# Cross attention in a two-layer decoder: six rounds a row of four 125-key units, in place of eight rounds of one head pair

## The reference

```python
Q = (x @ Wq.T).reshape(B, xN, NUM_HEADS, HEAD_DIM)
KV = (z @ Wkv.T).reshape(B, zN, 2, NUM_HEADS, HEAD_DIM)
attn = jnp.einsum('bqhd,bkhd->bhqk', Q, K) * SCALE
attn = jax.nn.softmax(attn, axis=-1)
O = jnp.einsum('bhqk,bkhd->bqhd', attn, V).reshape(B, xN, DIM)
return O @ Wo.T
```

## Time and profile before

| | |
|---|---|
| median of 3 runs | 1423.16 us |
| profiled execution, its own time | 1427.28 us |
| its span | 1425.5 us |
| PE busy, PEld busy | 1253.4 us (88%), 1003.8 us (70%) |
| DVE, ACT, POOL busy | 703.0, 556.0, 444.4 us |
| first cross attention, second | about 153 to 468 us, 918 to 1226 us |

### The profile page before, as it was taken

The page is one execution under the profiler, slowest core; times in us unless marked ns, Lnnn a source line. Parts: engine busy times, 40 slices in busy tenths (PEclk is TensorE's granted clock), DMA queues, the critical chain, the costliest instruction groups (busy, mean ns, idle before and its releaser), DMA issues. The chain is left out here.

```text
span 1425.5 us, 34481 instructions
## 1 busy us (share of the span) xinstructions
PE 1253.4 (88%) x13524; PEld 1003.8 (70%) x13524; DVE 703.0 (49%) x1744; ACT 556.0 (39%) x1246; POOL 444.4 (31%) x654
## 2 busy tenths in 40 slices
PE   5999799999998199999994999789999999469996
PEld 2666467777776199999993777556777776369996
DVE  4786545555553622222222999655555555512332
ACT  2777145555554022222221555235555555112221
POOL 5986300000000246566552222200000000146562
PEclk9999799999999599999997999789999999779998
DMA  7000111111110379999994000011111111469993
GB/s 248 2 3 1 24 31 34 38 37 37 40 38 14 136 274 335 343 345 347 323 348 111 1 1 1 11 29 32 45 44 45 43 47 35 103 227 350 359 367 140
DMA packets 61355, 177.89 MB, mean 125 GB/s; under 512 B 20608, under 2 KB 41953, under 8 KB 46756
## 3 DMA queue, kind: packets, MB, share of 16 engines
q0 software_dynamic: 22176, 141.55, 27.8%
q1 hardware_dynamic: 39044, 34.46, 9.4%
HBM read 147.62 MB, written 12.85 MB: 113 GB/s over the span
## 5 line engine op out<-in xcount | busy, mean ns | idle before, releaser
L1010 DVE TENSOR_REDUCE xa_mx<-xa_ps_s 112x2 f32<-112x750 f32 x246 | 231.5, 941 | 215.0 <-PE xa_ps_s L710 202.7
L927 ACT ACTIVATE xa_p<-xa_ps_p 125x672 f32<-125x672 f32 x244 | 178.2, 730 | 216.5 <-PE xa_ps_p L716 216.5
L716 PEld LDWEIGHTS xa_ps_p<-xa_qT,xa_kT 32*125 32x125 f32 x2928 | 184.8, 186 | 88.5 <-ACT xa_p L927 54.6
L716 PE MATMUL xa_ps_p<-xa_qT,xa_kT 32*125 32x112 f32 x2928 | 225.8, 285 | 21.9 <-DVE xa_mx L1010 10.0
L710 PE MATMUL xa_ps_s<-xa_kT,xa_qT 32*112 32x375 f32 x984 | 222.2, 528 | 2.1 <-DVE xa_mx L1010 2.1
L1842 PEld LDWEIGHTS ex_ps_h<-ex_xT,ew_w 128*128 128x128 f32 x1792 | 213.4, 196 | 4.8 <-issue 2.0
L1842 PE MATMUL ex_ps_h<-ex_xT,ew_w 128*128 128x128 f32 x1792 | 213.9, 279 | 1.3 <-ACT ex_xT L1872 1.3
L1853 PE MATMUL ex_ps_y<-ew_w,ex_hT 128*128 128x256 f32 x896 | 202.7, 380 | 0.0
L1853 PEld LDWEIGHTS ex_ps_y<-ew_w,ex_hT 128*128 128x128 f32 x896 | 166.2, 190 | 20.0
L1876 ACT ACTIVATE ex_hT<-ex_ps_h,ew_w 128x128 f32<-128x128 f32 x224 | 69.9, 363 | 281.9 <-PE ex_ps_h L1842 281.9
L1888 DVE TENSOR_SCALAR ex_hT<-ex_ps_h,ew_w 128x128 f32<-128x128 f32 x224 | 68.3, 347 | 163.4 <-PE ex_ps_h L1842 163.4
(11 more groups left out here) (305 smaller groups left out, 1977.5 us busy)
## 6 DMA issues: line engine op xcount, KB each, us to landing
xa_kT<-xa_kU SPq DMA_DIRECT2D x128, 93.8 KB, 2.2
xa_qT<-xa_qU SPq DMA_DIRECT2D x64, 56.0 KB
xn<-xa_x SPq DMA_DIRECT2D x32, 112.0 KB, 2.2
lin_yg<-ys SPq DMA_DIRECT2D x16, 224.0 KB, 5.7
cT<-in_ctxT SPq DMA_DIRECT2D x4, 750.0 KB, 8.3
xa_qT<-xa_nmT SPq DMA_DIRECT2D x128, 1.8 KB
x<-in_x SPq DMA_DIRECT2D x4, 448.0 KB, 5.8
xn<-x SPq DMA_DIRECT2D x16, 112.0 KB, 2.1
```

Of the source, the lines that this page charges most:

```text
L716: return pe.matmul(shifted_banks(b, pair)[0:CT, i, c * S:(c + 1) * S], kT[r:r + 32, b % RB, n, c * CT:(c + 1) * CT], qT[r:r + 32, b % RB, ...
L927: act.activation(p[slot % 4][:, :, :], shifted_banks(t, slot)[0:CT, :, 0:NC3 * S], ACT.Exp).then_inc(exped, 1)
L1010: dve.tensor_reduce(mx[:, b % 2, j:j + 2, n], score_banks(b, pair)[0:S, :, 0:CL], AX, ALU.max).then_inc(maxed, 1)
```

## The change

- A row has six rounds. A round takes four units of 125 keys from each of two strips: `unit(slot, u)` numbers the twelve (quad, chunk) units of a strip, four to a slot. `score` multiplies one unit (125 columns) and no longer all 375; `shifted_score` is the product it was, eight to a round in place of six. `exps` covers 2 x 448 columns, into one of six tiles `p`.
- `maximum` leaves a maximum for each unit (48 a query), and `shift_rows` has a second reduction (`top`) from 48 to 16, ahead of the negation.
- `values` runs two groups at a time: 0 and 1 after round 4, 2 and 3 after round 0 of the next row, with a round on either side.
- The whole-array work stands after rounds 1, 2, 3 and 5. `logits` writes to bank `bm` and not to `bk`, so `keys` no longer waits for VectorE's `row_logits`; `finish` runs one row earlier. `queries` and the first `keys` are a row further ahead, and SP's spreading with them.
- The work ahead of the loop is written out anew: `x_turn(1)`, `queries(1)` and `keys(1, 0)` stand before the first `fill_round`; nine fill rounds in place of eleven.

```diff
-    PAIRS = H // 2
+    ROUNDS, UNITS = 6, 4
...
+    p = [ph.sb(f"p{r}", [CT, 2, UNITS * S]) for r in range(ROUNDS)]
+    mx = ph.sb("mx", [S, 2, 4, QUADS * NC3])
+    top = ph.sb("top", [S, H])
...
+    AHEAD = 3
+    FILL = ROUNDS + AHEAD
+    DRAIN = ROUNDS * NB - FILL
+    EXPED = (2, 4, 6, 6)
...
+    def unit(slot, u):
+
+        k = UNITS * (slot // 2) + u
+        return k // NC3, k % NC3
...
+                n, c = unit(slot, u)
+                return pe.matmul(score_banks(b, slot)[0:S, i, u * CT:(u + 1) * CT], qT[r:r + 32, b % RB, n, :],
+                                 kT[r:r + 32, b % RB, n, c * CT:(c + 1) * CT], start=True, stop=True)
...
             def round_of(t, slot):
                 sb, sp = ahead(t, slot)
...
+                    spread_waits(sb, sp)
+                    r = ROUNDS * sb + sp
+                    pe.wait_ge(maxed, r)
+                for u in range(UNITS):
+                    if on(t):
+                        for i in range(2):
+                            last = shifted_score(t, slot, i, u)
+                        if u == UNITS - 1:
+                            last.then_inc(shifted, 1)
+                    if on(sb):
+                        for i in range(2):
+                            last = score(sb, sp, i, u)
+                        if u == UNITS - 1:
+                            last.then_inc(scored, 1)
...
+                    k = NC3 * n + c
+                    u = k % UNITS
                     for j in range(4):
+                                         p[2 * (k // UNITS) + j // 2][:, j % 2, u * S:(u + 1) * S], start=(c == 0), stop=(c == NC3 - 1))
...
             def x_turn(b):
                 pe.wait_ge(x_normed, b + 1)
...
                 reused(pe, nm_copied, b - 1)
...
             def logits(b):
                 pe.wait_ge(x2_t, b + 1)
+                pe.wait_ge(x_summed, min(b + 2, NB))
...
-                    last = pe.matmul(bk[0:S, 2 * P:2 * P + NE], x2T[:, c, :], g.wr[:, layer, c, :], start=(c == 0), stop=(c == 1))
+                    last = pe.matmul(bm[0:S, 2 * P:2 * P + NE], x2T[:, c, :], g.wr[:, layer, c, :], start=(c == 0), stop=(c == 1))
...
             def keys(b, m):
+                reused(pe, k_copied, 2 * b + m)
                 if m == 0:
-                    reused(pe, k_copied, 2 * b)
-                    reused(pe, lg_set, b - 4)
-                else:
-                    reused(pe, v_copied, NC3 * b)
-                    pe.wait_ge(k_copied, 2 * b + 1)
+                    reused(pe, v_copied, NC3 * (b - 2) + 2)
+                    reused(pe, x2_t, b - 4)
...
             for t in range(NB + 2):
                 round_of(t, 0)
                 if on(t - 1):
+                    values(t - 1, 2)
                     values(t - 1, 3)
-                if on(t + 2):
-                    keys(t + 2, 0)
...
                 round_of(t, 1)
-                if on(t + 2):
-                    queries(t + 2)
-                round_of(t, 2)
-                if on(t):
-                    values(t, 0)
-                if on(t - 1):
-                    u_turn(t - 1)
-                round_of(t, 3)
-                if on(t + 1):
-                    context_values(t + 1, 0)
-                    context_values(t + 1, 1)
-                round_of(t, 4)
-                if on(t):
-                    values(t, 1)
-                if on(t + 1):
-                    context_values(t + 1, 2)
-                round_of(t, 5)
                 if on(t + 2):
                     keys(t + 2, 1)
                 if on(t + 1):
-                    shift_turn(t + 1)
-                round_of(t, 6)
-                if on(t):
-                    values(t, 2)
+                    context_values(t + 1, 0)
+                if on(t - 1):
+                    u_turn(t - 1)
+                round_of(t, 2)
+                if on(t + 1):
+                    context_values(t + 1, 1)
+                    context_values(t + 1, 2)
                 if on(t - 1):
                     out_turn(t - 1)
-                if on(t - 2):
-                    row_turn(t - 2)
-                round_of(t, 7)
-                if on(t + 3):
-                    x_turn(t + 3)
+                round_of(t, 3)
+                if on(t + 1):
+                    shift_turn(t + 1)
                 if on(t - 1):
                     out_product(t - 1)
                 if on(t - 2):
+                    row_turn(t - 2)
+                if on(t + 3):
+                    x_turn(t + 3)
+                round_of(t, 4)
+                if on(t):
+                    values(t, 0)
+                    values(t, 1)
+                round_of(t, 5)
+                if on(t + 3):
+                    queries(t + 3)
+                    keys(t + 3, 0)
+                if on(t - 2):
                     logits(t - 2)
...
-                act.wait_ge(shifted, PAIRS * t + slot + 1)
-                reused(act, valued, 4 * t + slot // 2 - 1)
-                act.activation(p[slot % 4][:, :, :], shifted_banks(t, slot)[0:CT, :, 0:NC3 * S], ACT.Exp).then_inc(exped, 1)
+                act.wait_ge(shifted, ROUNDS * t + slot + 1)
+                reused(act, valued, 4 * t - (2 if slot < 2 else 0))
+                act.activation(p[slot][:, :, :], shifted_banks(t, slot)[0:CT, :, 0:UNITS * S], ACT.Exp).then_inc(exped, 1)
...
                     out_copy(t - 1)
+                if on(t):
+                    exps(t, 3)
+                if on(t + 1):
+                    shift_copy(t + 1)
                 if on(t - 2):
                     row_copy(t - 2)
                 if on(t + 3):
                     x_copy(t + 3)
+                if on(t):
+                    exps(t, 4)
+                    exps(t, 5)
+                if on(t + 3):
+                    k_copy(t + 3, 0)
...
+            def maximum(b, slot):
+                dve.wait_ge(scored, ROUNDS * b + slot + 1)
+                j, k = 2 * (slot % 2), UNITS * (slot // 2)
+                made = score_banks(b, slot)[0:S, :, 0:UNITS * CT].rearrange("t i (u k) -> t i u k", u=UNITS)
+                dve.tensor_reduce(mx[:, b % 2, j:j + 2, k:k + UNITS], made, AX, ALU.max).then_inc(maxed, 1)
...
             def shift_rows(b):
-                dve.wait_ge(maxed, PAIRS * (b + 1))
+                dve.wait_ge(maxed, ROUNDS * (b + 1))
+                made = mx[:, b % 2].rearrange("t j (n c) -> t (j n) c", c=NC3)
+                dve.tensor_reduce(top[:, :], made, AX, ALU.max).then_inc(topped, 1)
...
+                    if slot == 1 and on(t - 2):
                         second_norm(t - 2)
...
+                    if slot == 2 and on(t + 1):
                         shift_rows(t + 1)
+                    if slot == 3 and on(t - 1):
+                        finish(t - 1)
+                    if slot == 5 and on(t + 3):
+                        q_copy(t + 3)
+                    if slot == 5 and on(t - 2):
+                        row_logits(t - 2)
...
```

More of the change, by code:

```diff
@@ L731, in round_of @@
[L731 to L734, removed]
-                if on(t):
-                    for i in range(2):
[L737 to L740, removed]
-                if on(t):
[L742 to L745, removed]
@@ L756, in values, with fill_round @@
+            def fill_round(b, slot):
+                spread_waits(b, slot)
+                reused(pe, maxed, ROUNDS * b + slot - 1)
+                for u in range(UNITS):
+                    for i in range(2):
+                        last = score(b, slot, i, u)
+                last.then_inc(scored, 1)
             def values(b, n):
-                pe.wait_ge(exped, PAIRS * b + 2 * n + 2)
+                pe.wait_ge(exped, ROUNDS * b + EXPED[n])
                 if n == 0:
@@ L828, in u_turn @@
                 reused(pe, x_summed, b)
+                reused(pe, lg_set, b - 1)
                 for n in range(QUADS):
@@ L857, in _ @@
             keys(0, 1)
+            x_turn(1)
             bias_rows()
-            idle_products(bp[:, 0, 0:P], 5 + 4 * layer)
+            queries(1)
+            keys(1, 0)
+            idle_products(bp[:, 0, 0:P], 2)
             fill_round(0, 0)
             fill_round(0, 1)
-            x_turn(1)
-            keys(1, 0)
+            keys(1, 1)
+            context_values(0, 0)
             fill_round(0, 2)
             fill_round(0, 3)
-            queries(1)
+            context_values(0, 1)
+            context_values(0, 2)
             fill_round(0, 4)
             fill_round(0, 5)
-            context_values(0, 0)
-            context_values(0, 1)
-            fill_round(0, 6)
-            fill_round(0, 7)
-            context_values(0, 2)
-            keys(1, 1)
+            fill_round(1, 0)
             shift_turn(0)
-            for pair in range(FILL - PAIRS):
-                fill_round(1, pair)
+            keys(2, 0)
             x_turn(2)
+            fill_round(1, 1)
+            fill_round(1, 2)
+            queries(2)
             for t in range(NB + 2):
@@ L970, in _ @@
```

(27 more changed lines are left out.)

172 lines of the change are left out of this document (73 added, 99 removed).

## The result

The changed kernel takes 1389.91 us (median of 4 runs, 1389.60 to 1390.92) against 1424.91 (1421.94 to 1428.47): a ratio of 0.9755, 95% interval 0.9729 to 0.9781. The forecast was 1387. The profiled span is 1387.9 us, 37.6 less than before.

What follows compares the result with a forecast made beforehand. It took each gap as bound by VectorE's loop or TensorE's round plus work. 28 rows x 1.24 = 34.7, 1.2 for rows 14 and 4 for layer 0's waits: 39.9 off 1427.28, forecast 1387 us, range 1368 to 1409.

Steps and rivals of the forecast that it cites:

- Two paces: Cross-attention rows: each round-to-round gap lasts the longer of VectorE's loop (2.55 us) or the round (1.06) plus TensorE's work behind it.
- Gap 3: From round 3's start to the next round: `x_turn` waits for ScalarE's copy of the turned maxima, 2.85 us.
- The gaps: Times from round n's start to the next round's, six a row: together 16.47 us against 17.71, 1.24 less.
- gap 5: After round 5: the round, then `queries`, `keys` and `logits`, 1.06 + 2.15 = 3.2 us.
- gap 1: After round 1: the round, then `keys`, `context_values` and `u_turn`, 1.06 + 1.71 = 2.77 us.
- The start: Work and fill rounds ahead of each layer's loop: taken at nothing, bounds +2 and -3 us a layer.
- Row 14's wait and the drain: End of the layers: 1.2 us less for two rows 14, 4 for layer 0's DMA waits; drain exponentials equal.
- Instructions: Feeding TensorE about 325 products a row, up from 262: taken at nothing, priced between nothing and 0.4 us a row.
- the slower rival: TensorE's instructions can't be fed, deciding from 54 ns a product: 1473 to 1477 us; chance 0.09, 0.06 for feeding.
- no change: Round 0 waits for the turned maxima's late DMA; at 3.7 us delay time stays near 1423 us; chance 0.08.
- smaller gain: Products of four strips step at 0.12 or 0.13 us, not 0.11: 1399 to 1411 us; chance 0.18.
- larger gain: The round takes its lower bound (13 us) or the start its own (6 us): 1381 to 1368 us; chance 0.05.

Runs made afterwards that it cites:

- half_max_after: The changed kernel with VectorE's maximum over 500 of 1000 elements and the exponential's argument scaled by 0.01; only rows compared, a row takes 15.50 us.
- rebalance_after: The changed kernel with `row_turn` moved to the gap after round 2 and `logits` to the one after round 3: 1382.51 us, ratio 0.9706.

## Why the prediction was right

- **Two paces:** as said, and the loop's share is shown by half_max_after. Round 1.06, step 0.11, maximum 1.20, exponential 0.92 (0.91 said); loop 2.58 (2.55 said). Gap 3 has a third pace, ScalarE's copy, which the prediction had too.
- **The gaps**, from round 0 on, measured against said: 2.58 (2.55), 2.75 (2.77), 2.58 (2.55), 2.67 (2.85), 2.58 (2.55), 3.08 (3.2). The row is 16.25 where 16.47 was said, and 28 rows saved 39.4 us, not 34.7. Two terms were too large. In gap 3 the wait of `x_turn` for the copy came as said, but earlier: the exponential ends 2.09 us after the round and not 2.2, the copy is drawn from 0.11 us before that end and is done at 2.22, not 2.44. In gap 5 the prediction's own prices (0.9, 0.63, 0.40) add up to 1.93 and not to the 2.15 it used; measured are 0.99, 0.64 and 0.40. In gap 1 they add up to 1.63 and not 1.71; there 1.69 was measured.
- **The start** was the mis-sized term: "I take nothing, with +2 and -3 us a layer as bounds". It cost 4.8 and 3.3 us in the profiled execution. I had counted maxima, where the first score itself came later: 13.59 us after the first product for 10.05 in layer 0, 12.54 for 10.81 in layer 1. 1.55 and 1.53 us of that are a wait of `x_turn(1)` for VectorE's normalised row, which I had at nothing; the rest is what the added steps take, in part at half clock, less the idle products that are no longer there. Then came 13.7 us at half clock in place of 6.8, from the last fill rounds into row 0. "Its clock [...] may stay up" was the wrong way round: the granted clock of row 0 fell from 0.82 to 0.79 in layer 0 and from 0.84 to 0.81 in layer 1, that of the stretch ahead from 0.84 to 0.73 and from 0.77 to 0.68. The wait in layer 0:

```profile
159.94 0.42 PE L797 MATMUL xa_ps_x<-ident,xa_xn 112*128 112x112 f32 x2 [1.55 <-DVE xa_xn L178]
```

- **Row 14's wait and the drain:** 1.2 + 4 us said, 4.9 + 1.2 measured.
- **Luck in the total:** the rows gave 4.7 us more than said, the starts took 8.2 that were put at nothing, row 14 and the rest gave 1.2 more. 37.6 us for the 39.9 said is near because these errors cancel but for 2 us; a right total didn't prove the terms.
- **Instructions** cost nothing: 325 products in 16.25 us are 50 ns each, 48 with the short maxima, 28 within a pair of value groups (48 in 1.34 us). So TensorE was fed faster than the 54 ns at which the slower rival begins. The Trainium skill ("TensorE: Matmul & The Clock Gate", "Wait — 56ns, not 53.3ns?") gives about 62 ns for each matmul where hardware decode is off. The 50 ns of this trace show that this is not the price here; no run shows which way decode stood. The copy of the turned maxima starts at 291.68 and they are used at 298.04; no round of the loop waited for their DMA. So fell "no change"; "smaller gain" fell with the step of 0.11, "larger gain" with the round of 1.06 and the start.

## What to carry to other kernels

Where engines alternate, write down for each gap which one ends it: work put where another engine sets the pace is free (`row_turn` in VectorE's gap 2, `logits` before the `x_turn` that waits for ScalarE), and shortening one engine pays only in its own gaps. To see whether a product waited, look at its weight load as well: the matmul rows of gap 3 show no idle time. Put products of one kind behind one another; here a group of values alone among whole-array products cost 0.3 us more than behind another group. Cost a stage's start by its own rows and at the clock that it had there, and not by the loop's pace.

## What had not been expected

The clock at the start differed between two layers that run the same order (1.00 and 0.51 behind the same wait of 1.21 us), and row 0 took 15.74 and 18.84 us there. It differed between executions of one order too: layer 1's row 0 had 0.81 in the changed kernel's run and 1.00 in rebalance_after's. This is the likely reason why a first score 4 us sooner gained nothing until it came with idle products ahead of it, but one execution of each was profiled, and what decides the clock there was not found.
